# Projection and seeds by quadrants, a 256 KB chain for the large adapter weight

## The chip, the cores and the metric

The kernel runs on one core of one Trainium2 chip. The metric is the device time of one execution in microseconds (us), lower is better. Engines are named as in the profile: PE is TensorE (PEld its weight loads), DVE VectorE, ACT ScalarE, POOL GpSimd, SP SyncE, which here only issues DMAs. A DMA issue keeps its engine's queue busy for some tenths of a microsecond; landing is when the transfer's semaphore has its value.

## The reference

Inputs are `x` (16 sequences, 256 tokens, 256 features), `cond` (16 x 256) and weights, all f32. Two layers, each added to its input:

```python
# layer 0: an LSTM over the 256 tokens, hidden size 256, h0 = cond, c0 = 0
xz = einsum('ntd,dk->ntk', x, Wx) + b
z = xz_t + prev_h @ Wh                    # gates i, f, o, g
next_c = sigmoid(f) * prev_c + sigmoid(i) * tanh(g)
next_h = sigmoid(o) * tanh(next_c)
x = x + hs
# layer 1: an adapter whose four low-rank factors (rank 8) are made from cond
c = layernorm(cond) * ln_gamma + ln_beta
w = gelu(c @ W1 + bias1) @ W2 + bias2     # 256 x 8192: W2 is 8 MB
a1, b1, a2, b2 = split(w, 4)              # each per sequence, 256 x 8
u = x @ a2
mid = gelu(x @ base_down + u @ b2.T)
out = mid @ base_up.T + a1 @ (b1.T @ mid)
x = x + out
```

## The kernel before

**Recurrence.** The 256 time steps run one after the other, unrolled, in 32 blocks of `TB` = 8 steps (I call them steps 0 to 255 and blocks 0 to 31). In a step PE adds `h @ Wh` to what lies in PSUM already (L677): 16 sequences fill 16 partitions, and the hidden units are spread over four quadrants of 32 partitions (j = 0 to 3), so that each group of four narrow matmuls writes beside one another. Units are split in two halves m; gates i, f, g of a half lie in `z_bank[m]`, gate o of both in `o_bank`. DVE turns 32 x 32 tiles (L830, L834), ACT takes tanh, DVE forms cell and hidden state (L840, L845, L855), and PE starts the next step. In the gaps PE does all other work of the kernel: one eighth of the projection of a block ahead, a part of the adapter of a block behind (`follower`, from block 3 on), and in the first blocks the making of the adapter weights.

**Projection and seeds.** `project` (L463) multiplies 128 tokens of x (8 steps x 16 sequences) by `wx`, in 8 pieces: four parts q of 256 columns by two halves of the contraction. Part q is gate q. `evacuate_projection` (L761) adds the bias `b_all` and scatters each gate over the four quadrants of `proj` (`gate_cols`). When all four gates are there, SP moves `proj` into `seed` by four DMAs, one for each quadrant (`load_seed`, L249). In every step ACT copies the step's slice of `seed` into the PSUM banks (`seed_bank`, `seed_o`) before PE accumulates.

**Start.** PE does `WARM_UP` = 4 matmuls on zeros, turns the first x block, and spreads the bias `b` over all partitions by two 512-column matmuls with one row of ones (L634). It projects block 0 (waits for the wx loads and the bias), turns `cond` for the first hidden state, projects half of block 1, and starts step 0 when ACT has put in the seeds. ACT doubles the g columns of `wx` and `wh` (`double_g`).

**Adapter weights.** `W2` is needed in four quarters of 2 MB, in the order `QUARTERS`; each is one DMA (`load_w2`, L275). Three tiles hold them; the fourth waits until the first quarter is used up (L305). SP's queue works in the order of the program: its block 0 has x, the second quarter, the seeds of block 2 (they wait until the seeds of block 0 are consumed), the third quarter. Each of the steps 7 to 22 (`W_FIRST` = 7) has one piece of the product on PE (L606), a piece being one half of a quarter's columns by one half of the contraction; it needs its quarter whole. Every second step DVE adds the bias tile `w_bias` (L882), and when a quarter is ready POOL issues four DMAs that place it (`place_w`, L970). POOL also loads `w_bias` by four DMAs at the start (L963), and adds x and h for the adapter (`add_h`, L943); its queue has `add_h` of a block ahead of the `place_w` calls of that block.

Of the kernel before, what the change touches and what calls it, by code (L numbers as in the profile page):

```python
# [20 lines left out]
ALU = mybir.AluOpType  # L21
ACT = mybir.ActivationFunctionType
# [3 lines left out]
G = 4  # L26
P = 128
# [14 lines left out]
W_FIRST = 7  # L42
# [12 lines left out]
WARM_UP = 4  # L55


def lstm_adapter(nc, x, cond, Wx, Wh, b, base_up, base_down, gamma, beta, W1, bias1, W2, bias2, out):
    ctx = ExitStack()
    with ctx:  # L60
# [6 lines left out]
        def sem(name):  # L67
# [5 lines left out]
        ones = sb("ones", [P, P])  # L73
# [3 lines left out]
        b_row = sb("b_row", [1, G * H])  # L77
# [64 lines left out]
        consts_made = sem("consts_made")  # L142
        zeroed = sem("zeroed")
        w_loaded = {n: sem(f"{n}_loaded") for n in
                    ("wx_if", "wx_og", "wh", "b", "down", "up", "ln", "cond", "w1")}
        w2_loaded = [sem(f"w2_loaded{q}") for q in range(4)]
# [39 lines left out]

        def gate_cols(t, gate):

            quadrants = t[:, :].rearrange("p (j n) -> p j n", n=ZW)
            if gate == 2:  # L190
                return quadrants[:, :, NM * GC:ZW].rearrange("p j (m c) -> p m j c", c=C)
            place = {0: 0, 1: 1, 3: 2}[gate]
            return quadrants[:, :, 0:NM * GC].rearrange("p j (m g c) -> p g m j c", m=NM, c=C)[:, place]
# [48 lines left out]
        def _(sp):  # L242
# [6 lines left out]
            def load_seed(f):  # L249
# [23 lines left out]
            w2_q = W2.rearrange("(k p) (q n) -> q p k n", p=P, q=4)  # L273
# [5 lines left out]
            sp.dma_start(b_row[:, :], b.rearrange("(a n) -> a n", a=1)).then_inc(w_loaded["b"], 16)  # L279
            load_cols(wx, Wx, 0, 0, 2 * H, "wx_if")  # L280
            load_cols(wx, Wx, 2 * H, 2 * H, 2 * H, "wx_og")
            sp.dma_start(c_in[:, :], cond).then_inc(w_loaded["cond"], 16)
            load_cols(wh, Wh, 2 * H, 3 * H, H, "wh")
            load_cols(wh, Wh, 0, 0, 2 * H, "wh")
            load_cols(wh, Wh, 3 * H, 2 * H, H, "wh")
# [9 lines left out]
            load_w2(QUARTERS[0])  # L295
# [713 lines left out]
```

## Time and profile before

| what | before |
| --- | --- |
| median of 3 runs (lowest, highest) | 606.96 us (605.89, 607.08) |
| time of the profiled execution | 607.91 us |
| its span, first to last instruction | 605.7 us |
| PE, PEld busy | 586.7 us (97%), 437.7 us (72%) |
| DVE, ACT, POOL busy | 501.5 us (83%), 384.6 us (63%), 49.7 us (8%) |
| mean granted PE clock | 0.994 |
| DMA moved | 39.74 MB, mean 66 GB/s |

The profiled execution took 2.2 us more than its span and 0.95 us more than the median. The page also gives the chain of work that ended last, followed back from the last instruction: 95% PE, then issue, DMA, DVE and POOL with 1% each. "issue" is time in which an engine waited for nothing that the profile shows. A matmul of f32 stands in the records as two, a transpose as one.

### The profile page before, as it was taken

Reading aid. Unit: us, or ns where it says so; the run is one execution under the profiler, and the core shown is the slowest. Engines: PE = TensorE matmul, PEld = TensorE weight load, DVE = VectorE, ACT = ScalarE, POOL = GpSimd, SP = SyncE. Lnnn points to the kernel's source line nnn. Section 1 sums busy time; section 2 is a strip of 40 time slices with the busy share of each in tenths; the row PEclk is TensorE's granted clock in tenths of the full one; section 3 lists DMA queues with packets and bytes.
Section 4 is the critical chain, followed back from the end, with each engine's and each line's share of the span. In section 5 each row is a group of like instructions: output and inputs, shape, how many; then the busy total and the mean of one; then the engine's idle time right before and its main releaser. Section 6 shows DMA issues by size and latency. Waiting matters only on the chain.

```text
span 605.7 us, 34198 instructions
## 1 busy us (share of the span) xinstructions
PE 586.7 (97%) x14092; PEld 437.7 (72%) x14092; DVE 501.5 (83%) x2805; ACT 384.6 (63%) x2154; POOL 49.7 (8%) x96
## 2 busy tenths in 40 slices
PE   8698999999999999999999999999999999999997
PEld 5564567777777777777777777777777777777885
DVE  2577888888888888888888888888888888888873
ACT  1365566666666666666666666666666666666673
POOL 5001320000000000000000000000000000000000
PEclk9799999999999999999999999999999999999999
DMA  7889340232323113233311232322133233113201
GB/s 193 218 219 311 68 56 15 36 55 56 56 56 52 32 31 56 55 56 56 56 32 28 56 55 56 55 47 39 29 57 55 55 56 53 34 30 45 56 21 29
DMA packets 32142, 39.74 MB, mean 66 GB/s; under 512 B 3906, under 2 KB 29810, under 8 KB 30963
## 3 DMA queue, kind: packets, MB, share of 16 engines
q1 hardware_dynamic: 31282, 36.51, 30.3%
q8 instruction: 112, 1.84, 1.4%
q0 software_dynamic: 704, 1.05, 1.2%
q14 instruction: 44, 0.35, 0.2%
HBM read 16.05 MB, written 4.19 MB: 33 GB/s over the span
## 4 chain that ended last, share of the span: by engine, by line
PE 95%; issue 1%; DMA 1%; DVE 1%; POOL 1%; SPq 0%; ACT 0%; POOLq 0%; ACTq 0%
PE z L677 36%; PE x_bank L481 19%; PE z_o L677 9%; PE aux L507 8%; PE out_bank L531 7%; PE aux L492 3%; PE aux L459 3%; PE out_bank L563 2%; PE aux L514 2%; PE out_bank L606 1%; DMA seed<-proj 1%; PE out_bank L552 1%; PE x_bank L552 1%; DMA x_nat<-in_x 0%; PE x_bank L507 0%
## 5 line engine op out<-in xcount | busy, mean ns | idle before, releaser
L677 PE MATMUL z<-wh,h_t 128*16 128x96 f32 x8160 | 235.3, 249 | 3.5 <-issue 3.1
L677 PEld LDWEIGHTS z<-wh,h_t 128*16 128x16 f32 x8160 | 153.2, 96 | 109.5 <-DVE h_t L855 79.6
L830 DVE STREAM_TRANSPOSE z<-z 128x96 f32<-128x96 f32 x512 | 152.8, 299 | 73.3 <-PE z L677 47.6
L404 ACT ACTIVATE gates<-z 128x48 f32<-128x48 f32 x512 | 108.1, 211 | 122.6 <-DVE z L830 122.3
L481 PE MATMUL x_bank<-wx,x_t 128*128 128x256 f32 x512 | 156.3, 393 | 0.5 <-ACT x_t L336 0.5
L342 ACT ACTIVATE z<-seed 128x96 f32<-128x96 f32 x512 | 127.0, 248 | 5.8 <-DMA seed<-proj 5.8
L677 PE MATMUL z_o<-wh,h_t 128*16 128x64 f32 x4080 | 104.9, 219 | 0.1
L840 DVE SCALAR_TENSOR_TENSOR prod<-gates 128x32 f32<-128x32 f32 x512 | 98.7, 193 | 0.0
L481 PEld LDWEIGHTS x_bank<-wx,x_t 128*128 128x128 f32 x512 | 81.3, 197 | 5.9 <-issue 1.5
L677 PEld LDWEIGHTS z_o<-wh,h_t 128*16 128x16 f32 x4080 | 80.0, 97 | 0.6 <-issue 0.5
L346 ACT ACTIVATE z_o<-seed 128x64 f32<-128x64 f32 x256 | 58.4, 228 | 19.3
L952 POOL TENSOR_TENSOR xp<-x_t,h_t 128x128 f32<-128x128 f32 x60 | 30.4, 530 | 483.2 <-DVE h_t L855 449.1
L410 ACT ACTIVATE gate_o<-z_o 128x32 f32<-128x32 f32 x256 | 50.6, 198 | 27.1 <-DVE z_o L834 1.7
L834 DVE STREAM_TRANSPOSE z_o<-z_o 128x64 f32<-128x64 f32 x256 | 65.9, 257 | 0.2
L416 ACT ACTIVATE z_o<-z 128x16 f32<-128x16 f32 x256 | 43.0, 168 | 25.8 <-DVE z L845 0.4
L766 DVE TENSOR_TENSOR proj<-x_bank,b_all 128x256 f32<-128x256 f32 x128 | 54.1, 422 | 6.2 <-PE x_bank L481 6.0
L845 DVE SCALAR_TENSOR_TENSOR z<-prod 128x16 f32<-128x16 f32 x256 | 46.7, 182 | 8.7
L850 DVE SCALAR_TENSOR_TENSOR gates<-prod 128x32 f32<-128x32 f32 x256 | 47.2, 185 | 0.0
L416 ACT ACTIVATE tanc<-tanc 128x16 f32<-128x16 f32 x256 | 45.6, 178 | 0.2
L855 DVE SCALAR_TENSOR_TENSOR h_t<-gate_o,z_o 128x16 f32<-128x16 f32 x256 | 43.7, 171 | 0.2
L855 DVE SCALAR_TENSOR_TENSOR h_t<-gate_o,tanc 128x16 f32<-128x16 f32 x256 | 43.7, 171 | 0.0
L507 PE MATMUL aux<-xp,down 128*128 128x128 f32 x232 | 43.3, 289 | 0.0
(125 smaller groups left out, 518.9 us busy)
## 6 DMA issues: line engine op xcount, KB each, us to landing
seed<-proj SPq DMA_DIRECT2D x128, 128.0 KB, 4.4
w<-in_L_cond_W SPq DMA_DIRECT2D x4, 2048.0 KB, 10.6
x_nat<-in_x SPq DMA_DIRECT2D x32, 128.0 KB, 4.3
out<-y_nat SPq DMA_DIRECT2D x32, 128.0 KB, 4.2
wx<-in_L_cond_Wx SPq DMA_DIRECT2D x2, 512.0 KB, 4.9
wh<-in_L_cond_Wh SPq DMA_DIRECT2D x2, 256.0 KB, 6.6
wh<-in_L_cond_Wh SPq DMA_DIRECT2D x1, 512.0 KB, 5.8
w_bias<-in_L_cond_bias POOLq DMA_DIRECT2D x4, 128.0 KB, 6.8
```

The lines of the kernel that those rows point to most:

```text
L342: act.activation(z_bank[m][:, 0:GC], seed[buf][:, s, GC * m:GC * (m + 1)], ACT.Copy)\
L346: act.activation(o_bank[:, 0:OC], seed[buf][:, s, NM * GC:ZW], ACT.Copy).then_inc(seeded_o, 1)
L404: act.activation(gates[s % 2][m][:, 0:3 * B].rearrange("p (g b) -> p g b", b=B), zt[m].rearrange("p (g c) -> p g c", c=C)[:, :, 0:B], ACT. ...
L416: act.activation(tanc[m], cell[m], ACT.Tanh, scale=0.5).then_inc(tanc_ready[m], 1)
L481: ins = pe.matmul(x_bank[q % 2][:, 0:XW], x_t[f.k % N_X][:, kc, :], wx[:, kc, q * XW:(q + 1) * XW], start=(kc == 0), stop=(kc == 1))
L507: ins = pe.matmul(mid_bank[a.lane][:, cols], lhs, rhs, start=(part == 0), stop=(part == 2))
L677: ins = pe.matmul(dst, h_prev[:, kc, :], rhs, start=False, stop=(kc == 1), skip_group_check=True)
L766: dve.tensor_tensor(gate_cols(proj[f.par], q), x_bank[q % 2][:, 0:XW].rearrange(units, m=NM, c=C), b_all[:, q * XW:(q + 1) * XW].rearrange ...
L830: dve.transpose(zt[m], z_bank[m][:, 0:GC]).then_inc(turned[m], 1)
L834: dve.transpose(zt_o, o_bank[:, 0:OC]).then_inc(turned_o, 1)
L840: dve.scalar_tensor_tensor(prod[m][:, :], now[:, 0:2 * B], 1.0, now[:, 2 * B:4 * B], ALU.add, ALU.mult).then_inc(prod_ready[m], 1)
L855: dve.scalar_tensor_tensor(h_t[k.par][:, m, s, 0:B], gate_o[:, B * m:B * (m + 1)], 1.0, tanc[m], ALU.add, ALU.mult).then_inc(ht_ready[m], 1)
```

## The change

It has these parts.

- **Bias.** `b` goes into row 0 of a zeroed 128-row tile `b_pad`, issued from ACT's queue, as `cond` is. Its spreading is now eight matmuls of 128 rows by 128 columns into two banks, against a tile whose first row holds 2 or 4, with the result in quadrant order; DVE copies it.
- **Projection.** Part q is now quadrant q with all four gates: the matmul reads `wx` in runs of 32 columns, and DVE's evacuation and the seed copy are contiguous. Block 0's projection waits for all of `wx`. Block 1's has six of its eight pieces ahead of step 0.
- **Seeds.** Each of the four seed DMAs waits for its own quadrant only. `seed_o` reads two runs of 32.
- **Start.** `WARM_UP` = 6; another matmul on zeros behind the `cond` transposes; these come ahead of bias and projection. The loads of Wx and Wh have the g columns first. The third x block is turned in step 1.
- **W2.** 16 parts (a piece's own data) of two halves of 64 partitions: 32 DMAs of 256 KB. Each waits until the one three before it has landed. They start behind the loads of the start; block 0 of SP's queue has parts 0 to 7, block 1 parts 8 to 12, block 2 parts 13 to 15, between x loads and seeds. The four DMAs of `w_bias` stand on SP's queue behind parts 2 to 5.
- **Pieces.** `W_FIRST` = 11: the pieces run in steps 11 to 26, the last three in block 3. The turning of placed weights moves from steps 0 and 4 of block 2 to 2 and 6. POOL places quarter 0 after `add_h` of block 0, quarters 1 and 2 after that of block 1, quarter 3 after that of block 2. The waits for the placed weights stand later in `down_full` and `up_full`.

```diff
-W_FIRST = 7
+W_FIRST = 11
+UNDER_WAY = 3
-WARM_UP = 4
+WARM_UP = 6
 # SP: seeds and W2
-                sp.wait_ge(xz_ready, f.k * XQ + XQ)
                 for j in range(NQ):
+                    sp.wait_ge(xz_ready, f.k * XQ + (j + 1))
                     sp.dma_start(seed[f.par][32 * j:32 * j + B, :, :], proj[f.par][:, ZW * j:ZW * (j + 1)])\
                       .then_inc(seed_loaded[f.par], 16)
-            def load_w2(q):
-                sp.dma_start(w2[q][:, :, :], w2_q[q]).then_inc(w2_loaded[q], 16)
+            def load_w2(piece):
+                n, i = divmod(piece, NQ)
+                q, (h, kc) = QUARTERS[n], divmod(i, 2)
+                if piece == 3 * NQ:
+                    sp.wait_ge(w_psum, 2)
+                for r, rows in enumerate((slice(0, P // 2), slice(P // 2, P))):
+                    back, half = divmod(2 * piece + r - UNDER_WAY, 2)
+                    if back >= 0:
+                        sp.wait_ge(w2_loaded[QUARTERS[back // NQ]][back % NQ][half], 16)
+                    sp.dma_start(w2[q][rows, kc, :].rearrange("p (j h n) -> p h j n", j=NQ, n=W_HALF)[:, h],
+                                 w2_parts[q, h, kc, rows]).then_inc(w2_loaded[q][i][r], 16)
-            load_w2(QUARTERS[0])
             load_seed(Blk(0, 1))
             load_cols(down, base_down, 0, 0, D, "down")
             def one_block(k, front):
+                if not k.at_least(1):
+                    load_w2(0)
+                    load_w2(1)
                 if k.plus(3).exists():
                     load_x(k.plus(3))
-                if not k.at_least(1):
-                    load_w2(QUARTERS[1])
-                if k.k == 1:
-                    sp.wait_ge(w_psum, 2)
-                    load_w2(QUARTERS[3])
+                for piece in {0: range(2, 8), 1: range(8, 13), 2: range(13, 4 * NQ)}.get(k.k, ()):
+                    load_w2(piece)
+                    if 2 <= piece < 2 + NQ:
+                        load_w_bias(piece - 2)
                 if front:
                     load_seed(k.plus(2))
-                if not k.at_least(1):
-                    load_w2(QUARTERS[2])
 # ACT: its two DMAs, the g columns, the seeds
+            act.dma_start(c_in[:, :], cond).then_inc(w_loaded["cond"], 16)
+            act.wait_ge(b_zeroed, 1)
+            act.dma_start(b_pad[0:1, :], b.rearrange("(a n) -> a n", a=1)).then_inc(w_loaded["b"], 16)
-                act.activation(o_bank[:, 0:OC], seed[buf][:, s, NM * GC:ZW], ACT.Copy).then_inc(seeded_o, 1)
+                act.activation(o_bank[:, 0:OC].rearrange("p (m c) -> p m c", c=C),
+                               seed[buf][:, s, :].rearrange("p (m q) -> p m q", m=NM)[:, :, GC:P], ACT.Copy)\
+                   .then_inc(seeded_o, 1)
 # PE: the projection and the bias
-                    ins = pe.matmul(x_bank[q % 2][:, 0:XW], x_t[f.k % N_X][:, kc, :], wx[:, kc, q * XW:(q + 1) * XW],
+                    ins = pe.matmul(x_bank[q % 2][:, 0:XW].rearrange("p (m g c) -> p m g c", m=NM, c=C),
+                                    x_t[f.k % N_X][:, kc, :],
+                                    wx[:, kc, :].rearrange("p (g m j c) -> p j m g c", g=G, m=NM, c=C)[:, q],
                                     start=(kc == 0), stop=(kc == 1))
+            for i, bank in enumerate((out_bank, tanc_bank)):
+                for place, gate in enumerate((0, 1, 3, 2)):
+                    quarters = bank[:, :].rearrange("p (j m g c) -> p g j m c", j=2, m=NM, c=C)
+                    ins = pe.matmul(quarters[:, place], rows_of[4 if gate == 3 else 2][:, :],
+                                    b_pad[:, gate * H:(gate + 1) * H]
+                                    .rearrange("p (m j c) -> p j m c", m=NM, c=C)[:, 2 * i:2 * i + 2],
+                                    start=(place == 0), stop=True, skip_group_check=True)
+                ins.then_inc(b_psum, 1)
+            project(Blk(0, 0), range(N_PIECES))
+            transpose_x(Blk(0, 1), both)
+            project(Blk(0, 1), range(6))
 # DVE: the evacuation
-                units = "p (m j c) -> p m j c"
-                dve.tensor_tensor(gate_cols(proj[f.par], q), x_bank[q % 2][:, 0:XW].rearrange(units, m=NM, c=C),
-                                  b_all[:, q * XW:(q + 1) * XW].rearrange(units, m=NM, c=C), ALU.add)\
-                   .then_inc(xz_ready, 1)
+                dve.tensor_tensor(proj[f.par][:, q * XW:(q + 1) * XW], x_bank[q % 2][:, 0:XW],
+                                  b_all[:, q * XW:(q + 1) * XW], ALU.add).then_inc(xz_ready, 1)
 # POOL
-                if k.k in (0, 1):
-                    place_w(2 * k.k)
-                    place_w(2 * k.k + 1)
+                for n in {0: (0,), 1: (1, 2), 2: (3,)}.get(k.k, ()):
+                    place_w(n)
```

## Rows read from the trace of the kernel before

**Rows 1.** Timeline, DVE: first cell update of steps 0, 1, 7, 8, 16, 24, 32, 240; start us, us.

```profile
24.32 0.14 DVE L845 SCALAR_TENSOR_TENSOR tanc<-prod 128x16 f32<-128x16 f32 x1
28.19 0.15 DVE L845 SCALAR_TENSOR_TENSOR tanc<-prod 128x16 f32<-128x16 f32 x1
...
41.65 0.14 DVE L845 SCALAR_TENSOR_TENSOR tanc<-prod 128x16 f32<-128x16 f32 x1
...
45.15 0.14 DVE L845 SCALAR_TENSOR_TENSOR tanc<-prod 128x16 f32<-128x16 f32 x1
...
66.63 0.37 DVE L845 SCALAR_TENSOR_TENSOR tanc<-prod 128x16 f32<-128x16 f32 x1
...
85.01 0.37 DVE L845 SCALAR_TENSOR_TENSOR tanc<-prod 128x16 f32<-128x16 f32 x1
...
103.50 0.14 DVE L845 SCALAR_TENSOR_TENSOR tanc<-prod 128x16 f32<-128x16 f32 x1
...
562.28 0.14 DVE L845 SCALAR_TENSOR_TENSOR tanc<-prod 128x16 f32<-128x16 f32 x1
```

**Rows 2.** Chain that ended last, in order of time, the start; start us, us, what.

```profile
4.24 2.00 PE out_bank L634 x2
...
7.94 6.54 PE x_bank L481 x16
...
17.00 4.70 DMA seed<-proj
...
22.18 1.48 PE z L677 x32
```

**Rows 3.** Timeline, PE at the start: warm-up matmuls, transposes of cond.

```profile
2.02 0.63 PE L625 MATMUL z_o<-zeros 128*128 128x96 f32 x2
...
2.45 0.63 PE L625 MATMUL z<-zeros 128*128 128x96 f32 x2
...
14.39 0.29 PE L639 MATMUL out_bank<-ident,c_in 16*128 16x16 f32 x2
```

**Rows 4.** Chain: projections of four records in step 0 and in step 2.

```profile
24.71 1.71 PE x_bank L481 x4
...
30.11 1.06 PE x_bank L481 x4
```

**Rows 5.** Windows of 2 us: busy us of each engine, PE clock, DMA share, GB/s.

```profile
20.00:22.00 2.00, 0.00 (x0) 0.00 (x0) 0.00 (x0) 0.22 (x2) 0.00 (x0) 0.64 1.10 171
22.00:24.00 2.00, 1.82 (x48) 1.67 (x48) 0.58 (x3) 0.71 (x5) 0.00 (x0) 0.50 1.17 407
```

**Rows 6.** DMA to landing us: of the seeds to 40 us, W2 (L276), base_up.

```profile
DMA to landing us min/median/max: 3.4/4.1/4.7
...
DMA to landing us min/median/max: 10.0/10.6/11.9
...
up_raw<-in_L_cond_base_up SPq DMA_DIRECT2D x1, 256.0 KB, 4.1
```

**Rows 7.** Chain: two stops of PE in block 1, and one weight piece.

```profile
53.07 1.38 issue
...
59.42 1.68 issue
...
62.30 0.56 PE out_bank L606 x8
```

**Rows 8.** DMA queues from 52 to 54 us: packets, MB, share of 16 engines.

```profile
q8 instruction: 1, 0.02, 3.3%
```

**Rows 9.** Chain in block 3: POOL's DMA issues, then what fills a step's gap.

```profile
82.23 1.35 POOL a_t L975 x3
...
92.25 0.64 PE aux L507 x4
92.89 0.43 PE x_bank L481 x2
...
94.11 0.22 PE z_o L677 x16
```

More of the change, by code:

```diff
@@ L72, in lstm_adapter @@
         zeros = sb("zeros", [P, P])
[L73 removed]
+        rows_of = {n: sb(f"row_{n}", [P, P]) for n in (2, 4)}
         gelu_0 = sb("gelu_0", [1, 1])
@@ L142, in lstm_adapter @@
         consts_made = sem("consts_made")
+        b_zeroed, rows_zeroed, rows_made = sem("b_zeroed"), sem("rows_zeroed"), sem("rows_made")
         zeroed = sem("zeroed")
         w_loaded = {n: sem(f"{n}_loaded") for n in
-                    ("wx_if", "wx_og", "wh", "b", "down", "up", "ln", "cond", "w1")}
-        w2_loaded = [sem(f"w2_loaded{q}") for q in range(4)]
+                    ("wx_g", "wx_if", "wx_o", "wh_g", "wh_if", "wh_o", "b", "down", "up", "ln", "cond", "w1")}
+        w2_loaded = [[[sem(f"w2_loaded{q}_{i}_{r}") for r in range(2)] for i in range(NQ)] for q in range(4)]
         w_bias_zeroed, w_bias_loaded = sem("w_bias_zeroed"), sem("w_bias_loaded")
@@ L430, in one_block @@
                         seed_o(ahead.par, s_next)
-                    if s == 0 and not k.at_least(1):
+                    if s == 1 and not k.at_least(1):
                         evacuate_x(k.plus(2))
-                    if not k.at_least(EARLY + 1):
+                    if not k.at_least(EARLY + 2):
                         make_weights(k.k, s)
@@ L601, in make_weights @@
                         pe.wait_ge(w_biased, 2 * n + h)
-                    if i == 0:
-                        pe.wait_ge(w2_loaded[q], 16)
+                    for half in w2_loaded[q][i]:
+                        pe.wait_ge(half, 16)
                     for j in range(NQ):
@@ L609, in make_weights @@
                         ins.then_inc(w_psum, 1)
-                if k == 2 and s in (0, 4):
+                if k == 2 and s in (2, 6):
                     n = s // 4
@@ L821, in _ @@
             dve.tensor_scalar(c_stat[:, 3:4], c_stat[:, 2:3], 1.0 / D, LN_EPS, ALU.mult, ALU.add).then_inc(ln_step, 1)
-            for q in range(2):
+            for q in range(XQ - 1):
                 evacuate_projection(Blk(0, 1), q)
@@ L871, in make_weights @@
                        .then_inc(cond_t_ready, 1)
-                if k > 0 and s % 2 == 0:
-                    u = ((k - 1) * TB + s) // 2
+                u, between = divmod(k * TB + s - W_FIRST - 1, 2)
+                if 0 <= u < 2 * NQ and not between:
                     n, h = divmod(u, 2)
@@ L917, in one_block @@
                         add_residual(done)
-                    if not k.at_least(1) and s < 2:
-                        evacuate_projection(Blk(0, 1), 2 + s)
+                    if s == 0 and not k.at_least(1):
+                        evacuate_projection(Blk(0, 1), XQ - 1)
                     if front and k.at_least(1) and s in EVACUATE_AT:
@@ L960, in _ @@
             pool.wait_ge(w_bias_zeroed, 1)
-            bias_q = bias2.rearrange("(q j n) -> j q n", q=4, j=NQ)
-            for j in range(NQ):
-                pool.dma_start(w_bias[32 * j:32 * j + B, :, :], bias_q[j].partition_broadcast(B))\
-                    .then_inc(w_bias_loaded, 16)
             pool.wait_ge(ln_step, 6)
```

113 lines of the change are left out of this document (56 added, 57 removed).

## The prediction

> **What bounds the kernel now.** I read first the page's chain by engine (95% PE), then the first cell update of each step, which gives the pace. From step 32 to step 240 a step takes (562.28 - 103.50)/208 = 2.206 us, a block 17.65. The first four blocks take 20.83, 21.48, 18.38 and 18.49: together 79.18 where four even blocks are 70.6, so 8.6 us too much [rows 1]. Ahead of them the first recurrent matmul starts only at 22.18 [rows 2]. So all that this change can win lies in the first 104 us: a start of 22 us and 8.6 us of disturbance. The other 500 us are even, and there a step is balanced: z_o 0.22, adapter 0.64, projection 0.43 and the z matmuls just fill the 2.2 us until the next hidden state [rows 9]; any work added to a PE gap of a block with a follower costs its whole time.
>
> The start, from the chain: the bias spreading 4.24 to 7.94, the projection of block 0 until 14.48, an evacuation, four seed DMAs one after the other, of which the last is issued at 17.00 and lands 4.70 later, ACT's seeds, first matmul at 22.18 [rows 2]. PE runs at the low clock for most of it: 16 records in 6.54 us are 0.41 each, as 1.71/4 = 0.43 in step 0, where the granted clock is 0.50 (1.2 GHz), and not 1.06/4 = 0.265 as in step 2 [rows 2, 4, 5]. (The windows view writes 1.00 for the start; the records show otherwise.) PE then idles until 22, the clock falls to 0.50 in that idle time, and steps 0 and 1 pay again: 3.87 us from the update of step 0 to that of step 1 [rows 1, 5].
>
> The disturbance: step 7 to 8 takes 3.50 us instead of 2.2, and two more stops of 1.38 and 1.68 in block 1 are "issue", in the middle of a run of matmuls that wait for nothing [rows 1, 7]. They fall where the 2 MB transfers of W2 fill the DMA engines, 10 to 12 us each [rows 6], and in the window of one of them stands exactly one packet of the instruction queue [rows 8]. I read them as PE out of instructions, whose fetch came late behind W2.
>
> **The change part by part.**
>
> *PE's start.* Two more warm-up matmuls at 0.43 (2.02 to 2.45): the eight records end at 3.08, twelve end at 3.9 [rows 3]. The x transposes and the two of cond (0.29) follow, then one matmul on zeros: 5.3. The bias is 16 records of 128 columns. By columns (four records of 512 took 2.00 + 1.71 before) 16 take 3.7 at the low clock; by the adapter's records of 128 columns (0.64/4 = 0.16 at the full clock) 16 take 2.6 at the full and 5.1 at the low clock [rows 2, 9]. I take 3.9, end at 9.2: 1.3 later than now. That hides the new wait for all of Wx, which is there at about 7.8 now and is issued earlier in the new order; ACT's doubling of g as well.
>
> *Projection of block 0.* Now PE works with full 128-row matmuls without a stop from 1.06, before it had one-row matmuls until 7.94. I expect the clock to be up by about 10 us. Then 16 records take 3 x 0.41 + 13 x 0.265 = 4.7: end at 13.9. Bounds: all high and the bias at 2.6, 5.3 + 2.6 + 4.25 = 12.2; all low, 5.3 + 4.3 + 6.54 = 16.1.
>
> *Seeds.* Three of four are gone before the last evacuation; the last is issued at 13.9 + 0.5 = 14.4 (before 17.00). Landing 3.4 to 4.7, median 4.1 [rows 6]; I take 4.4, and 0.45 for ACT: first recurrent matmul at 19.25 instead of 22.18, **-2.9 us**. Bounds 16.6 (-5.6) and 21.8 (-0.4).
>
> *Clock in steps 0 and 1.* PE's new gap: the projection of block 1 has 12 records (3.2 us) and waits for the layernorm arithmetic on DVE (about 2 us); PE ends near 17.8 and idles 1.5 us instead of 4.6. I expect the clock to stay up. Step 0 to its first update then takes about 1.55 instead of 24.32 - 22.18 = 2.14, and 3.87 becomes 2.25, the step after it saves 0.15 [rows 1, 2]: **-2.35**. Bounds: 0 (it falls again) and -2.5.
>
> *W2 in 256 KB transfers.* At most 768 KB is queued instead of 2 MB and more. In the even part the four seed DMAs queue 512 KB each block, and the steps stay at 2.206, so a backlog of that size costs no stop. I take the three stops as gone: 1.3 in step 7 and, of block 1's excess of 3.8, all but 0.5 that its extra work costs, 3.3: **-4.6** [rows 1, 7]. Bounds -4.6 and 0, as several later fetches fall beside W2 now.
>
> Here pages of the Trainium skill speak against me. "Runtime: NRT & Kernel Launch", section "Instruction fetch mechanics", says that fetches come in blocks of 16 KiB, which the one packet of 0.02 MB bears out [rows 8], but also that PE holds 128 KiB of instructions and that fetching is mostly hidden; and "DMA: Bandwidth & Descriptors", "Anatomy of one DMA", says that a DMA engine takes its queue rows in turn, packet by packet. By these a long queue of W2 would hardly delay a fetch, and the stops would stay; that is rival A below, worked out there from rows.
>
> *Is W2 in time?* The first transfer is issued when the last seed of block 1 and base_down are out, about 22.5. 256 KB landed in 4.1 [rows 6]; with three under way one lands each 1.37 us. First landing 26.6, the other 31 take 42.5, and SP's other issues between them (12 seeds, 4 bias, 3 x, 0.6 each = 11.4), half hidden in the waits, 5.7: last landing at 74.8. Its piece is due in step 26, at 19.25 + 26 x 2.21 + 1.7 = 78.4. So it is in time by 3.6. The pieces between need 2.2 us each and get 2.7, but start 18 us ahead. The seeds of blocks 2 to 4 have a block of slack. Cost nothing, hidden by the steps; if the cover goes, see rival C.
>
> *Pieces in steps 11 to 26.* 13 of 16 stay in blocks without a follower, where a step with a piece runs at about 2.2 already. Three fall into block 3, in gaps that are full: 3 x 0.56 = +1.7 [rows 7, 9]. Against it, POOL's DMA issues no longer stand ahead of its x plus h (1.35 us of the chain) and step 24 loses its 0.75 of delay [rows 9]. The turnings move at no cost. Net **+0.9**, bounds 0 and +1.7.
>
> *Every step after.* Evacuation, seed copies and the reordered `wx` reads keep their sizes. z_o already reads `wh` in runs of 32 columns: 16 records in 0.22 are four groups of 64 columns, 0.86 ns a column; the projection has 0.43/512 = 0.84 [rows 9]. I take 0; see rival D. The seed DMAs of later blocks have a block of slack.
>
> **Sum:** -2.9 - 2.35 - 4.6 + 0.9 = -8.95. Span 605.7 - 8.95 = 596.75; the execution, with 2.2 around it, 599.0 instead of 607.91; against the median of 606.96, which is 0.95 lower, 598.0.
>
> **Rivals.** A: the stops stay, since the fetch is late for another reason or DMA is busy for longer now: -8.95 + 4.6 (less what step 7 no longer meets, 0.5) = -4.9, 602.1. For it: more fetches fall beside W2. Against: the even part beside the seeds.
> B: the clock stays low through bias and projection, or falls in the gap: +2.4 on either, 600.4. "TensorE: Matmul & The Clock Gate", Part 4, says that transposes don't count as work for the clock; that would favour this.
> C, on the other side: W2 arrives too slowly. Place: PE at L606, from the part that lands after its step on. If a transfer takes t each (other issues in it), the last lands at 26.6 + 31 t, due 78.4: PE starts to wait from t = 1.67. At t = 1.95 it is 8.7 late, the gain is used up; at 2.1, 13.3 late, 611.3. For it: halves of 64 partitions in rows of 1 KB, and a chain that pauses for each landing and for SP. Against: 2 MB in 10.6 is 1.3 for 256 KB, though without pauses.
> D: the projection's reads in runs cost PE time. 8.95/256 = 0.035 us a step uses up the gain, 8% of 0.43; at twice that 607 + 9 = 616. Against: z_o's columns.
>
> **Numbers.** Forecast 0.64 (596 to 600.5), A 0.12, B 0.12, C 0.08, D 0.04. The predicted time is 598.0. The range has to reach A and the better bounds of the start: 594.5 to 603. A measurement of this kernel tells about 0.2% (1.2 us) from no change. Faster: forecast, A, B and the mild part of C, 0.87; same 0.03; slower 0.10.
>
> **What would show it.** First recurrent matmul near 19.3; records of L481 at 0.265 from about 10 us on, and no 0.50 of the clock after; steps 7, 11, 13 at 2.2 to 2.3, no "issue" above 0.5 in blocks 0 to 2; steps 24 to 26 at about 2.7; blocks from 4 on at 17.6. Wrong would be: blocks above 17.7 (D), L606 waiting for DMA (C), stops at other steps (A), 0.41 a record past 11 us (B).

## The result: a third of the forecast gain

| | before | after |
| --- | --- | --- |
| median (lowest, highest; runs) | 606.70 us (604.68, 607.80; 6) | 603.68 us (603.16, 604.24; 6) |
| profiled execution, its span | 607.91, 605.7 | 603.59, 601.6 |
| blocks 0, 1, 2, 3 | 20.83, 21.48, 18.38, 18.49 | 19.70, 21.96, 20.29, 18.80 |

The ratio is 0.994 [0.9921, 0.996]: faster by 3.0 us (the two spans differ by 4.1), where 8.95 were forecast. 603.68 lies just above the range of 594.5 to 603. A block is counted from the first cell update of one block to that of the next.

The page of the kernel after, its head, busy times and chain by engine:

```profile
span 601.6 us, 34256 instructions
...
PE 582.8 (97%) x14110; PEld 438.2 (73%) x14110; DVE 502.3 (83%) x2809; ACT 384.6 (64%) x2154; POOL 47.4 (8%) x91
...
PE 92%; DMA 3%; DVE 2%; issue 1%; SPq 0%; ACT 0%; POOL 0%; POOLq 0%; ACTq 0%
```

DMA has 3% of the chain instead of 1%: that is new. Timeline, DVE, of the kernel after, first cell update of steps 0, 1, 8, 15, 16, 24, 32, 240 (start us, us), against [rows 1]:

```profile
19.14 0.14 DVE L870 SCALAR_TENSOR_TENSOR tanc<-prod 128x16 f32<-128x16 f32 x1
...
21.48 0.14 DVE L870 SCALAR_TENSOR_TENSOR tanc<-prod 128x16 f32<-128x16 f32 x1
...
38.84 0.15 DVE L870 SCALAR_TENSOR_TENSOR tanc<-prod 128x16 f32<-128x16 f32 x1
...
55.51 0.15 DVE L870 SCALAR_TENSOR_TENSOR tanc<-prod 128x16 f32<-128x16 f32 x1
...
60.80 0.14 DVE L870 SCALAR_TENSOR_TENSOR tanc<-prod 128x16 f32<-128x16 f32 x1
...
81.09 0.14 DVE L870 SCALAR_TENSOR_TENSOR tanc<-prod 128x16 f32<-128x16 f32 x1
...
99.89 0.14 DVE L870 SCALAR_TENSOR_TENSOR tanc<-prod 128x16 f32<-128x16 f32 x1
...
558.11 0.14 DVE L870 SCALAR_TENSOR_TENSOR tanc<-prod 128x16 f32<-128x16 f32 x1
```

By differences: the first update comes 5.18 earlier, block 0 takes 1.13 less, block 1 0.48 more, block 2 1.91 more, block 3 0.31 more, and steps 32 to 240 take 458.22 instead of 458.78 (2.203 a step, before 2.206). With the ends of the spans that is -4.1. One interval stands out: step 15 to 16 takes 60.80 - 55.51 = 5.29. The chain of the kernel after, in order of time (start us, us, what), says why:

```profile
5.35 1.98 PE out_bank L657 x8
7.33 1.71 PE tanc L657 x8
9.04 3.48 PE x_bank L491 x16
...
12.99 4.22 DMA seed<-proj
...
17.70 0.89 PE z L701 x32
...
24.36 0.28 issue
...
35.30 0.74 issue
...
47.08 0.62 issue
...
52.07 0.51 SPq L252
...
52.62 5.46 DMA x_nat<-in_x
...
58.13 0.44 PE aux L472 x2
...
70.94 7.37 DMA x_nat<-in_x
```

Two things are to be seen. The stops ("issue") are shorter, 0.27 to 0.74 instead of 1.38 and 1.68 [rows 7] (and 0.68 in step 7), but there are more of them: the steps in which they fall (2, 4, 6 and 11) take 2.64, 2.88, 3.06 and 3.05. And PE twice waits for an x load: for block 4 in step 15, for block 5 in step 23 (0.98 us). A stop of 0.27 and the turning of placed weights fall into steps 22 and 23 too; these two take 3.41 and 3.28. The first wait in the PE timeline (3.13 us, ended by that DMA):

```profile
58.13 0.44 PE L472 MATMUL aux<-ident,x_nat 128*128 128x128 f32 x2 [3.13 <-DMA x_nat<-in_x]
```

SP's queue, which issues it (timeline, SP: start, us until the last of the group is out), shows the load of block 4 at 52.62 behind four seeds and the chained W2 transfers, and that of block 5 behind ten of them:

```profile
43.10 5.79 SPq L279 DMA_DIRECT2D w<-in_L_cond_W  x4
49.06 3.52 SPq L252 DMA_DIRECT2D seed<-proj  x4
52.62 0.60 SPq L241 DMA_DIRECT2D x_nat<-in_x  x1
53.27 14.90 SPq L279 DMA_DIRECT2D w<-in_L_cond_W  x10
68.34 2.56 SPq L252 DMA_DIRECT2D seed<-proj  x4
70.94 0.61 SPq L241 DMA_DIRECT2D x_nat<-in_x  x1
71.60 10.31 SPq L279 DMA_DIRECT2D w<-in_L_cond_W  x6
```

DMA issues of W2 in the kernel after (landing; first and last issue):

```profile
DMA to landing us min/median/max: 3.4/5.2/8.3
...
L279 SPq DMA_DIRECT2D w<-in_L_cond_W x32: 595/596/1977, 21.6 to 81.3; - x32
```

So a transfer takes (81.3 - 21.6)/31 = 1.93 us, not 1.37. Last, the DMA queues from 36 to 41 us (packets, MB, share of the 16 engines), first of the kernel before, then of the kernel after:

```profile
q1 hardware_dynamic: 416, 1.96, 103.7%
```

```profile
q1 hardware_dynamic: 873, 0.94, 110.0%
```

The DMA engines are as busy as before while moving half as much. At most three 256 KB transfers of W2 are queued, beside seeds, x and the small `w_bias` loads (one is issued in these 5 us and one shortly before), but together they leave the engines no more room than two megabytes did. One window of 5 us depends on what else falls into it; the stretch of 22 to 62 us, which is compared further down, is the better measure.

### The profile page after: what moved, and what is told of

It reads as the page before. It is cut to its first block, busy times and chain, and to the rows that moved or that the text cites. A ratio compares the mean times of both kernels' runs of the same rounds, so it can differ in the third digit from the quotient of the medians.

```text
span 601.6 us, 34256 instructions
## 1 busy us (share of the span) xinstructions
PE 582.8 (97%) x14110; PEld 438.2 (73%) x14110; DVE 502.3 (83%) x2809; ACT 384.6 (64%) x2154; POOL 47.4 (8%) x91
## 4 chain that ended last, share of the span: by engine, by line
PE 92%; DMA 3%; DVE 2%; issue 1%; SPq 0%; ACT 0%; POOL 0%; POOLq 0%; ACTq 0%
PE z L701 35%; PE x_bank L491 17%; PE z_o L701 9%; PE aux L520 8%; PE out_bank L547 7%; PE aux L504 3%; PE aux L472 2%; PE out_bank L579 2%; PE aux L527 2%; DMA x_nat<-in_x 2%; PE out_bank L622 1%; PE out_bank L568 1%; DMA seed<-proj 1%; PE x_bank L568 1%; PE x_bank L520 0%
## 5 line engine op out<-in xcount | busy, mean ns | idle before, releaser
L701 PE MATMUL z<-wh,h_t 128*16 128x96 f32 x8160 | 234.6, 248 | 3.5 <-DVE h_t L880 1.9
L701 PEld LDWEIGHTS z<-wh,h_t 128*16 128x16 f32 x8160 | 153.1, 96 | 109.0 <-DVE h_t L880 80.4
L491 PE MATMUL x_bank<-wx,x_t 128*128 128x256 f32 x512 | 152.6, 385 | 0.6 <-ACT x_t L347 0.5
L701 PE MATMUL z_o<-wh,h_t 128*16 128x64 f32 x4080 | 105.0, 219 | 0.7 <-issue 0.7
L491 PEld LDWEIGHTS x_bank<-wx,x_t 128*128 128x128 f32 x512 | 78.8, 192 | 4.1 <-ACT x_t L347 0.7
L701 PEld LDWEIGHTS z_o<-wh,h_t 128*16 128x16 f32 x4080 | 80.2, 97 | 1.2 <-issue 0.9
```

Source lines behind the costliest of these rows:

```text
L491: ins = pe.matmul(x_bank[q % 2][:, 0:XW].rearrange("p (m g c) -> p m g c", m=NM, c=C), x_t[f.k % N_X][:, kc, :], wx[:, kc, :].rearrange("p ...
L701: ins = pe.matmul(dst, h_prev[:, kc, :], rhs, start=False, stop=(kc == 1), skip_group_check=True)
```

## The experiments

Each time stands beside the kernel before on the same chip (607.00 for the first four, then 608.03, 607.38 and 607.67 for four each, 606.87 for the last). The kernel after wasn't timed again beside them, so where microseconds are compared with its 603.68, the ratios (its own is 0.994) are the safer measure. Blocks, steps and chains are those of the one profiled execution, which is not always near the median: for x_ahead (605.98), by_columns_x_ahead (601.26) and columns_order_way4 (601.61) it was the slowest of their runs, for by_columns_first9 (599.37) the fastest.

| kernel | median us (runs) | ratio to before | blocks 0, 1, 2, 3 |
| --- | --- | --- | --- |
| x_ahead | 604.20 (10) | 0.9947 [0.9925, 0.9969] | 20.07, 20.30, 20.38, 22.13 |
| whole_quarters | 605.83 (10) | 0.9974 [0.9952, 0.9996] | 25.01, 18.63, 19.91, 19.09 |
| after_one_quarter | 598.75 (2) | 0.9857 [0.9798, 0.9916] | 18.96, 17.97, 19.21, 19.07 |
| before_one_quarter | 602.59 (8) | 0.9917 [0.9892, 0.9941] | 19.90, 17.89, 18.36, 18.62 |
| long_rows | 609.49 (10) | 1.0025 [1.0004, 1.0046] | 20.61, 19.05, 21.44, 23.76 |
| way6 | 616.16 (4) | 1.0143 [1.0081, 1.0206] | 22.34, 28.14, 23.39, 19.09 |
| long_rows_way2 | 617.31 (4) | 1.0160 [1.0114, 1.0205] | 18.07, 28.87, 23.66, 23.65 |
| bias_one_row | 605.86 (8) | 0.9975 [0.9941, 1.0008] | 17.91, 24.45, 20.35, 18.75 |
| **by_columns** | **598.42** (4) | 0.9843 [0.9819, 0.9868] | 18.41, 19.78, 19.86, 18.69 |
| by_columns_x_ahead | 599.38 (4) | 0.9859 [0.9824, 0.9894] | 17.99, 21.12, 20.07, 18.77 |
| by_columns_first9 | 601.41 (4) | 0.9895 [0.9866, 0.9924] | 18.25, 18.58, 20.78, 19.88 |
| parts_512 | 602.32 (4) | 0.9905 [0.9874, 0.9936] | 19.71, 20.57, 19.91, 19.08 |
| order | 603.73 (4) | 0.9923 [0.9898, 0.9949] | 20.06, 23.15, 19.18, 19.64 |
| columns_way5 | 601.97 (4) | 0.9895 [0.9863, 0.9927] | 21.09, 19.87, 18.84, 19.08 |
| columns_order | 599.72 (4) | 0.9870 [0.9836, 0.9904] | 18.07, 18.16, 19.66, 20.15 |
| columns_order_way4 | 600.44 (4) | 0.9865 [0.9831, 0.9900] | 20.26, 21.44, 18.85, 19.09 |
| columns_order_early | 599.59 (6) | 0.9872 [0.9845, 0.9898] | 17.92, 19.23, 20.36, 19.08 |

**The x loads one block earlier.**

```diff
-                if k.plus(3).exists():
+                if k.k in (0, 1):
+                    load_x(k.plus(3 + k.k))
+                    if k.k == 0:
+                        load_x(k.plus(4))
+                elif k.k > 2 and k.plus(3).exists():
                     load_x(k.plus(3))
```

> The kernel after, with the loads of x blocks 4 and 5 issued one block earlier on SP's queue, ahead of the W2 parts they stood behind; nothing else. Theory Q (SP's queue in order: the x loads wait behind chained W2 parts): the 3.1 us of step 15 and about 0.9 us of step 23 go, PE no longer waits for x_nat, 603.7 becomes 599.7. Rival S (the W2 supply itself is too slow, the x load only shows it first): W2 parts become late in their place, PE waits at the weight pieces, 602 to 604.

Measured 604.20: no gain. The x waits are gone, but step 15 still takes 3.87, step 23 4.22 and step 26 5.77. Its chain, in order of time, names the next in line:

```profile
35.51 1.01 issue
...
52.59 4.45 DMA seed<-proj
...
74.47 6.64 DMA w<-in_L_cond_W
...
81.13 6.59 DMA w<-in_L_cond_W
```

The seeds of block 2, then the last W2 parts, are late in x's place (PE waits 2.07 us for W2 in step 26). So the x wait was the first sign that SP's queue is late as a whole, and not a loss that can be taken away alone.

**W2 in four whole transfers again, all else as after.**

```diff
-                for piece in {0: range(2, 8), 1: range(8, 13), 2: range(13, 4 * NQ)}.get(k.k, ()):
-                    load_w2(piece)
...
+                if not k.at_least(1):
+                    load_w2(QUARTERS[1])
+                    for j in range(NQ):
+                        load_w_bias(j)
...
```

Each quarter is, as before the change, one DMA; the four `w_bias` loads now stand together behind the second quarter, where the kernel before had them on POOL's queue at the start.

> The kernel after, with W2 in four transfers of 2 MB without a chain, at the places they had in the kernel before; pieces still from step 11. Theory F (stops called issue are instruction fetches behind the queued W2): three or so stops of 1.3 to 1.9 us come back, the small ones of 0.3 to 0.8 go, the waits for x go: about 601 to 602. Rival N (the stops are not made by W2's queue): no large stops, small ones stay, x waits go: about 598 to 599.

Measured 605.83, above what either theory gave. Steps 4, 6 and 7 take 3.99, 6.29 and 3.35; from its chain, and the queue from 36 to 41 us:

```profile
29.34 1.41 issue
...
35.88 3.75 issue
```

```profile
q1 hardware_dynamic: 487, 0.60, 103.2%
```

So the new start with the old transfers has two stops in block 0 where the kernel before has one, and a longer one; a third of 1.00 us falls into step 20. Step 7 has no stop: PE sat idle for 3.75 us, the granted clock fell to 0.50 from 40 to 44 us, and the matmuls behind it ran at half rate. Nor was it W2 that filled the engines during most of the long stop: the queue moved 0.60 MB in those 5 us, and at most two of its 487 packets were W2's rows of 8 KB. The rest was mainly seeds and the `w_bias` loads, which go to 16 partitions each (the latter took 13.6 to 17.2 us to land, in the kernel after a median of 5.7). How much of the stop is theirs was not tested. The chained transfers are worth about 2 us net (ratios 0.9974 and 0.994, whose intervals overlap a little).

**Only one quarter of W2 loaded**, in the kernel after and in the kernel before.

```diff
-        w2 = {q: w2_tiles[n % 3] for n, q in enumerate(QUARTERS)}
+        w2 = {q: w2_tiles[0] for q in QUARTERS}
...
-                    load_w2(piece)
+                    if piece < NQ:
+                        load_w2(piece)
...
```

These are the lines of the kernel after; in the kernel before the three later `load_w2` calls are left out. In both, PE waits for the first quarter in place of its own.

> The kernel after, but only the first quarter of W2 is loaded and all four products read it, so three quarters of the adapter weights are not computed from their own data. Theory F and Q: from about 35 us on no stop of PE and no wait for x; steps 11, 15, 22, 23 at 2.2 to 2.6; about 597. Rival N: the stops of 0.6 in steps 11 and 22 stay, only the x waits go, 598.5.

> The kernel before, with the first quarter of W2 loaded alone and read by all four products, so three quarters of the adapter weights are not computed from their own data. Theory F: the stops of steps 7, 11 and 13 (4.6 us together) go, 606.7 becomes 602.1. Rival N (instructions are fetched well ahead whatever the DMA load): the stops stay at their places, 606 to 607.

Measured 598.75 and 602.59. In the first (two runs only), the one stop above 0.3 us (0.47) falls into block 0, while its quarter is loaded; later the steps take what the extra work of blocks 1 to 3 costs in the other kernels too, but for step 18 (2.91 instead of 2.56). In the second all three stops are gone and blocks 0 to 3 take 74.77 instead of 79.18. The stops come with W2's traffic: this is shown by taking it away from either kernel. The 4.4 us of the second are nearly the size that I gave that term (4.6).

**Rows of 8 KB, with three and with two under way.** Each 256 KB transfer goes to 32 partitions in whole rows instead of 64 partitions in rows of 1 KB.

```diff
-            w2_parts = W2.rearrange("(k p) (q j h n) -> q h k p j n", p=P, q=4, j=NQ, n=W_HALF)
+            w2_rows = W2.rearrange("(k g p) (q n) -> q k g p n", k=2, g=4, q=4)
...
+                    sp.dma_start(w2[q][32 * g:32 * g + 32, kc, :], w2_rows[q, kc, g]).then_inc(w2_loaded[q][kc][g], 16)
```

> The kernel after, with the same 32 chained transfers of 256 KB, three under way, at the same places of SP's queue, but each over 32 partitions with 8 KB a partition instead of 64 partitions with four pieces of 1 KB; x loads stay where they are. Theory R (short rows keep the DMA engines busy twice as long per byte): issue to landing falls from 5.2 to 3 or less, W2 is out by 60 us instead of 81, the waits for x in steps 15 and 23 go, the stops called issue get shorter; about 598 to 599. Rival L (the chain's pauses and landing latency set the pace): the pace stays 1.9 us a transfer and the x waits stay, 603 to 604.

> As long_rows, with two transfers under way. If the fetch stops follow the bytes queued, they get smaller than with three (a gain of up to 0.5 us) and the pace, about 1.3 us a transfer, is still enough: 598. If the pace drops to 1.7 or more, the x waits come back: 601 to 603.

Measured 609.49 and 617.31. Queue of long_rows from 36 to 41 us:

```profile
q1 hardware_dynamic: 258, 0.92, 104.7%
```

A third of the packets, the same bytes, nearly the same share: rows of 8 KB alone don't empty the engines. As the edit also halves the number of partitions, it doesn't clear the row length by itself; that needs the split by columns below, which keeps the rows at 1 KB. With two under way block 0 has no stop (18.07), and all else is late: step 15 takes 12.17 (PE waits 8.08 us for x), steps 23 and 24 7.26 and 7.34. These two kernels also need a whole quarter two steps sooner; what part that has was not measured.

**Six under way.**

```diff
-UNDER_WAY = 3
+UNDER_WAY = 6
```

> The kernel after, with six transfers under way instead of three. Theory R (the engines are full already): the pace stays near 1.9 us a transfer, landing doubles to about 10 us, x waits stay or grow, the stops called issue grow to 1 us and more: 604 to 607. Rival L: the pace goes to about 1.0, the x waits go: 599 to 600.

Measured 616.16. No x wait is left, but stops make six steps take 3.60 to 6.23. Windows of 22 to 62 us (busy us of each engine, clock, DMA share, GB/s), kernel after and way6:

```profile
22.00:62.00 40.00, 33.41 (x843) 22.43 (x846) 29.82 (x166) 22.86 (x130) 4.25 (x8) 1.00 0.91 178
```

```profile
22.00:62.00 40.00, 30.22 (x636) 21.08 (x628) 22.71 (x127) 17.70 (x101) 1.00 (x2) 0.84 1.09 198
```

Twice the backlog brings 11% more bytes and costs 12.5 us against the kernel after. A part of that is the clock: the four stops last 2.60 to 2.93 us, and behind each of them the granted clock is 0.50 (from 40 to 42, 50 to 52, 58 to 62 and 84 to 86 us). The stops of 1.38 and 1.68 in the kernel before left it at 1.00. The amount queued is a lever, as I had it; what I had wrong is how little may be queued in this form.

**The bias by one row** (as a test of the clock at the start).

```diff
-  rows_of[4 if gate == 3 else 2][:, :], b_pad[:, gate * H:(gate + 1) * H]
+  rows_of[4 if gate == 3 else 2][0:1, :], b_pad[0:1, gate * H:(gate + 1) * H]
```

> The kernel after, with the eight bias matmuls on one row instead of 128 (rows_of[0:1], b_pad[0:1]); same columns, same result. Theory K (full-array matmuls bring the clock up before the projection): the records of the bias keep 0.23 us, the projection of block 0 runs at 0.41 a record for most of it, 6 us instead of 3.5, first recurrent matmul 2 to 2.5 us later, total 605.5 to 606. Rival W (the two more warm-up matmuls and the unbroken run bring it up): no change, 603.7.

Measured 605.86. Its chain at the start:

```profile
9.06 5.34 PE x_bank L491 x16
...
14.88 3.68 DMA seed<-proj
...
19.05 0.89 PE z L701 x32
```

The projection of block 0 takes 5.34 us; in the other kernels whose bias has 128 rows it takes 3.47 to 4.49, and the first recurrent matmul starts at 16.69 to 18.56. The bias itself ends at the same time (9.06 against 9.04). So 128 rows of mostly zeros bring the full clock sooner, worth 0.9 to 1.9 us here, as far as one profile with one row against sixteen with 128 can tell. Most of its loss against the kernel after lies elsewhere, in step 15 (8.32): the x load of block 4 is out at 54.2 only, PE waits 4.2 for it, and behind that idle time the granted clock is 0.50 (58 to 62 us) and PE runs at half rate; behind the wait of 3.13 in the kernel after it stayed at 1.00. That is the wait of the kernel after with a worse outcome; whether the bias has a part in it, this one profile doesn't tell.

**Splitting a part by columns.** Both halves of a part now reach all 128 partitions, with two rows of 1 KB each; size, number, order and chain are untouched.

```diff
-                for r, rows in enumerate((slice(0, P // 2), slice(P // 2, P))):
+                for r, js in enumerate((slice(0, 2), slice(2, 4))):
...
-                    sp.dma_start(w2[q][rows, kc, :].rearrange("p (j h n) -> p h j n", j=NQ, n=W_HALF)[:, h],
-                                 w2_parts[q, h, kc, rows]).then_inc(w2_loaded[q][i][r], 16)
+                    sp.dma_start(w2[q][:, kc, :].rearrange("p (j h n) -> p h j n", j=NQ, n=W_HALF)[:, h, js],
+                                 w2_parts[q, h, kc, :, js]).then_inc(w2_loaded[q][i][r], 16)
```

> The kernel after, with each part's two transfers of 256 KB split by columns (two of the four 1 KB pieces in all 128 partitions) instead of by partitions (all four pieces in 64); bytes, piece length, order, chain of three and places are the same. Theory H (a transfer that writes few partitions fills the DMA engines at a fraction of the rate: 64 partitions about 180 GB/s, seeds over 16 partitions about 115, 2 MB over 128 partitions 400): landing falls from 5.2 to about 3, the last transfer is issued before 70 us, the x waits of steps 15 and 23 go, stops called issue shrink; about 598.5. Rival L2 (256 KB transfers in a chain don't go faster than about 180 GB/s however they lie): 603.7.

Measured 598.42 (597.88 to 599.05): the lowest median of all, 5.3 us below the kernel after, and as fast as the kernel that loads a quarter of W2. DMA of W2, chain (all of "issue" and DMA over 0.25 us from 20 to 80 us), queue from 36 to 41 us and window of 22 to 62 us of by_columns:

```profile
DMA to landing us min/median/max: 2.7/4.5/7.3
...
L279 SPq DMA_DIRECT2D w<-in_L_cond_W x32: 367/368/1979, 21.1 to 76.1; - x32
```

```profile
23.87 0.36 issue
...
49.19 4.91 DMA x_nat<-in_x
...
66.88 7.02 DMA x_nat<-in_x
```

```profile
q1 hardware_dynamic: 1104, 1.16, 85.2%
```

```profile
22.00:62.00 40.00, 36.02 (x929) 23.84 (x926) 33.03 (x184) 24.95 (x143) 4.28 (x8) 1.00 0.76 196
```

More bytes (196 GB/s against 178), at a share of 0.76 against 0.91: the engines have room again, the stops are gone but for one of 0.36, and a transfer takes 1.77 us instead of 1.93. The x waits remain (2.05 us in step 15, which takes 4.34, and 1.42 in step 23, which takes 3.69).

The total is the one that theory H gave (598.5), but not by its terms: landing fell to 4.5 and not to 3, the last transfer went out at 76.1 and not before 70, and the x waits did not go. Of the 4.5 us between the two spans, 0.5 lie ahead of the first update, 1.3 in block 0 and 2.2 in block 1, where the stops are gone and the x wait is 1.1 shorter, and 0.5 later. The pace of transfers with nothing between them hardly changed: ten took 14.31 instead of 14.90. SP is also held for less time by each issue (0.367 us instead of 0.595); which part of the earlier x load is due to that and which to the landing was not separated.

That the share falls with the split holds over all kernels. From 22 to 62 us queue q1 moves 6.86 MB in 87.5% of the engines' time in the kernel after and 7.58 MB in 73.4% in by_columns. Reckoned for 100%, the five kernels with halves of 64 partitions make 7.3 to 8.2 MB and the seven with 256 KB by columns 8.9 to 10.3. And the share goes with the stops: among the kernels with transfers of 256 or 512 KB, the six with a share of 0.85 or less in that stretch have no stop above 0.47 us, while in each of the ten with 0.89 to 1.09 the longest is 0.74 to 2.93 us. For 2 MB transfers this mean says little, as they come in bursts (0.85 in the kernel before, 0.72 in whole_quarters).

**Around by_columns.** One edit each: x one block ahead as above; the pieces from step 9 on (`W_FIRST = 9`); each part as one 512 KB transfer, two under way.

> by_columns with the x loads of blocks 4 and 5 one block earlier, as in x_ahead. Theory H: nothing is left to win by it, same as by_columns within 1 us. Rival L2: 604 as x_ahead.

> by_columns with the pieces in steps 9 to 24 instead of 11 to 26. If supply is no limit, two pieces of 0.5 us each leave block 3: 0.7 to 1.0 below by_columns. If W2 comes at 1.9 us a transfer, PE waits for parts from step 9 on and it is 2 to 4 us above.

> The kernel after, with each part as one transfer of 512 KB over 128 partitions and two under way. Theory H: supply at 2.6 us a part or better, no x waits; stops called issue like by_columns; 598 to 600. Rival L2: as L2 speaks of 256 KB, this one may be faster than by_columns by 2 us or more; under H they are the same within 1 us.

Measured 599.38, 601.41, 602.32: none better; the first can't be told from by_columns (its runs go from 597.50 to 601.26). In its profile, the slowest run, the seeds take x's place (step 15 takes 5.69). With earlier pieces PE waits 2.8 us for W2 in steps 22 and 24. With 1 MB queued the x waits go and stops come (four steps of blocks 0 and 1 take 2.79 to 3.48).

**SP's order and a longer chain.** In `order` the seeds of blocks 2 and 3 and the x loads stand further ahead in SP's queue:

```diff
-                if k.plus(3).exists():
+                if k.k in (0, 1):
+                    load_x(k.plus(3 + k.k))
+                elif k.k > 2 and k.plus(3).exists():
                     load_x(k.plus(3))
-                for piece in {0: range(2, 8), 1: range(8, 13), 2: range(13, 4 * NQ)}.get(k.k, ()):
+                for piece in {0: range(2, 6), 1: range(6, 12), 2: range(12, 4 * NQ)}.get(k.k, ()):
                     load_w2(piece)
...
+                    if piece == 3:
+                        load_x(Blk(0, 0, 4))
```

All the others split by columns. columns_way5 is by_columns with `UNDER_WAY` = 5 and the old order. columns_order is by_columns with the order above; columns_order_way4 adds `UNDER_WAY` = 4 to it, and columns_order_early puts parts 0 and 1 ahead of block 1's seeds.

> The kernel after (halves of 64 partitions, three under way) with another order of SP's queue: seeds of block 2 behind part 5 instead of 7, x 4 behind part 3, x 5 ahead of part 6, seeds of block 3 behind part 11. Theory Q (the waits for x and seeds are only SP's order): the waits of steps 15 and 23 go (4 to 5 us), 599. Theory H (the supply of W2 itself lacks time with full DMA engines): x and seeds are there, but parts 12 to 15 come late, PE waits at them in steps 23 to 26, 602 to 604.

> by_columns with five transfers under way, order as in the kernel after. Theory L (with the engines no longer full, the chain's landing latency of 4.5 us sets the pace): pace goes from 1.8 to about 1.3 us a transfer, the x waits of steps 15 and 23 (3.3 us) shrink to under 1, stops called issue come back by 1 to 2 us: 596.5 to 598. If the engines are full already: pace the same, stops larger, 600 to 602.

> by_columns with the order of the run order. The 2.1 us of step 15 and 1.2 us of step 23 go if the parts stay in time: 595 to 596. If parts 12 to 15 come late: 598.

> columns_order with four under way: parts are surely in time, stops called issue by up to 1 us more: 595 to 597; below columns_order if that one waits for its last parts.

> columns_order with parts 0 and 1 of W2 ahead of the seeds of block 1 on SP's queue, so that the chain starts near 16 us instead of 21.7. If the late parts are a late start: step 23 falls from 3.60 to 2.6, step 26 from 3.70 to 2.7, the seeds of block 1 are still there by step 7, no new stops: 2 us below columns_order, 597 to 598. If the pace at the end is the limit: steps 23 and 26 stay, 599.5. If the earlier traffic stops fetches in steps 0 to 3: 599 to 600.

Measured 603.73, 601.97, 599.72, 600.44, 599.59. In `order` no x or seed is waited for, and the chain has in step 13 (5.20 us) this stop:

```profile
51.94 2.89 issue
```

Behind it the granted clock is 0.50 from 56 to 58 us. Its time is that of the kernel after: here, in the form with halves of 64 partitions, the waits that were taken away came back as stops. With columns all four stay within 3.6 us of by_columns and none is better; the three with the new order are 1.2 to 2.0 us above it, and the intervals of their ratios overlap. Five under way make three steps of 3.44 to 4.16 with no x wait. The new order alone has no stop and no x wait, and moves the lateness elsewhere: in step 22 (3.60) PE waits 0.91 us for a placed weight (`w_tmp`), in step 26 (3.70) 0.97 us for a part of W2. Four under way and the earlier start end that and bring stops: in the first, steps of 3.05 to 4.70, in its slowest run; in the second, stops of 1.00 and 1.32 us.

## Why the prediction was right in direction and wrong in size

**The step that failed is "*Is W2 in time?*", costed at nothing.** Right was that PE does not wait for W2 in the kernel after. Wrong was what this was made to stand for: that the chain costs nothing. The step had 1.37 us for a transfer (4.1/3), 5.7 for SP's other issues, and "the seeds of blocks 2 to 4 have a block of slack"; for the x loads, which share that queue, it had no due time at all. Where SP issued ten transfers without anything between, they took 14.90, so 1.49 each: 31 are 46.2. The whole chain took 59.7, so the other issues, with SP's waits for DVE among them, cost 13.5, not 5.7: nothing of them was hidden in the waits. What SP waited for from 17 to 100 us in the kernel after (us in total, times, longest):

```profile
SPq L279 <- DMA w<-in_L_cond_W: 25.6, 19, 5.1
...
SPq L252 <- DVE proj L789: 4.5, 4, 2.5
```

The seeds wait for DVE's evacuation, and W2 and x stand behind them meanwhile. The last transfer went out at 81.3 where I had it landing at 74.8. PE never waited for W2, because the steps had slipped too (the last piece ran at 86.96, not 78.4); the lateness showed first at what stands behind W2 in the queue: 3.13 us in step 15 and 0.98 in step 23. Rival C had this mechanism and nearly its t (1.95), but its place was L606 and its price that of the last part. The mechanism was the right one, but what it delayed was the x load.

**The term that was over-counted: the stops, -4.6.** That they come with DMA traffic held (both one-quarter kernels, way6; whole_quarters too, though not all of its traffic was W2). What failed is "a backlog of that size costs no stop", taken from the seeds of the even part: there the DMA share is 0.28 on average (200 to 560 us), while the chain keeps it at 0.91 over the 40 us from 22 to 62. In the kernel after the stops still make three steps of block 0 (0.4 to 0.9 over 2.2), one of block 1 (0.85) and one of block 2 late.

By blocks, in us against the kernel before, forecast (from the terms) and measured: up to the first update -3.5 and -5.2; block 0 -3.1 and -1.1; block 1 -3.3 and +0.5; block 2 0 and +1.9; block 3 +0.9 and +0.3. So blocks 0 to 2 are 7.6 worse than forecast, and 2.8 of that doesn't show in the total, because the start, block 3 and the rest came out better. No term foresaw this, and that it hides a third of the miss is luck; the first update by itself varies by 1.9 us between profiles with the same start.

Against my own view I had set two pages of the Trainium skill, "Runtime: NRT & Kernel Launch", "Instruction fetch mechanics", and "DMA: Bandwidth & Descriptors", where the turn-taking of queue rows stands under "Queues, rings and completion order" and not in the section that I named. As I read them, the stops would stay whatever W2 does. This case's runs disagree: 607.00 to 602.59 with three quarters of W2 not loaded, and 603.68 to 616.16 with six transfers under way instead of three. So the first half of rival A, a fetch that is late for another reason, is out. Its second half, "DMA is busy for longer now", with stops at other steps as its sign, came true in part: the share from 22 to 62 us rose from 0.85 to 0.91, and the stops moved to steps 2, 4, 6 and 11. I had given A 0.12, and its 602.1 is nearer to the result than my forecast.

**What lies behind a large part of both:** by_columns changes neither order nor amount, and takes 5.3 us off. So that much is the price of splitting a part by halves of the partitions. That the kernel then takes what I forecast (598.42 for 598.0) is luck in part: its first update comes 5.69 earlier (18.63), where the terms of the start and of step 0 make 3.5, and PE waits 2.05 and 1.42 us for x, which I did not have.

**Right, or nearly.** *Clock in steps 0 and 1*: -2.35 forecast; the windows after show 1.00 from 18 us on, and update 0 to 1 takes 2.34 instead of 3.87 (1.53 less), with 0.89 for the 32 records at L701 instead of 1.48. *Start*: first recurrent matmul at 17.70, 4.5 earlier and not 2.9. The bias took 3.69 (3.9 forecast), the projection 3.48 instead of 4.7: at 0.22 a record, all of it at the full clock, so the clock rose by about 9 us. The sum of this term also took a wrong figure for the full clock: 0.265 a record from rows 4, where the 0.43 for two in rows 9 give 0.215; sixteen of these are 3.4. The seeds took 4.22 (4.4). *Block 3*: 0.3 more, 0.9 forecast. *Every step after*: 2.203, so the reads in runs of 32 columns cost nothing, and D is out. B is out too.

**Open.** That transfers over few partitions hold the DMA engines longer for the same bytes is measured (64 and 32 partitions alike, 128 not), but why is not, nor what part the length of the rows has: 2 MB in rows of 8 KB over 128 partitions, in the kernel before, make 12.4 MB for 100% of the engines' time from 22 to 62 us, more than any kernel with rows of 1 KB. Nor is it known how a fetch waits behind a full engine, or if there is an order of SP's queue with columns that has neither stops nor late loads: five tries each had one or the other, four of them at a time whose interval overlaps that of by_columns.

## What to carry to other kernels

A chain that bounds what is queued is no bound on how busy the DMA engines are: look at the share of the engines over such a stretch, beside GB/s, and split a large transfer by columns, with all 128 partitions in each piece, before making it smaller or its chain longer. Small loads to few partitions count in it too. Whatever stands in the same issuing queue behind chained transfers inherits their pace, so give every load in that queue a due time, the small ones first. And undo one wait only together with the next in line: x, seeds, W2 parts and instruction fetches here took each other's place at a nearly unchanged total (x_ahead, order). A stop can cost twice, once for itself and once for the low clock behind it; look at the granted clock behind the longest ones.

## What the runs showed of the hardware

- **Partitions per transfer.** 256 KB into 64 partitions (rows of 1 KB) or into 32 (rows of 8 KB) fill the 16 engines at 0.94 and 0.92 MB in 5 us; into 128 partitions (rows of 1 KB) 1.16 MB take 85%; 2 MB into 128 partitions (rows of 8 KB) reach 1.96 MB at 104%, with other loads of these kernels among them. From 22 to 62 us, for 100% of the engines' time: 7.3 to 8.2 MB with 64 partitions, 8.9 to 10.3 with 128 and rows of 1 KB. SP was also held for 367 ns by an issue with columns, against 595 with halves.
- **Instruction fetch behind DMA traffic.** PE stops in the middle of matmuls that wait for nothing, for 0.68 to 1.68 us with 2 MB transfers queued, for 3.75 when `w_bias` and seed loads stood behind these, for 0.27 to 0.74 beside three of 256 KB in 64 partitions and 0.36 beside three in 128. That these stops are late instruction fetches is a reading: what is measured is that they come with DMA traffic and go with it.
- **The clock.** With 128-row matmuls from the start on, PE's 16 projection records from 9.04 us on take 0.22 us each, as at the full clock (2.4 GHz) in the even part, and 0.33 on average behind a one-row bias. The view of the granted clock doesn't show this: it reads 1.00 from the start on in both. It read 0.50 behind idle times of 3.75 us (whole_quarters), 2.89 (order) and 4.2 (bias_one_row), and 1.00 behind those of 1.38, 1.68 (before) and 3.13 (after). The first cell update of kernels with the same start still varies from 18.1 to 20.0 us from one profile to the next.
